# Four value units move from the value projection to the end of the head stage, and four groups of gates stand five units apart

## The chip, the cores and the metric

The kernel runs on one core of a Trainium2 chip. A core has TensorE (PE in the rows; its weight loads are PEld), VectorE (DVE), ScalarE (ACT), GpSimd (POOL) and SyncE (SP), each with its own instruction stream, which meet at semaphores, and 16 DMA engines. The metric is the device time of one execution in microseconds; lower is better.

## The reference, cut to what matters

Two transformer layers work on 16 sequences of 128 tokens with 512 features. In the first layer an mLSTM with 16 heads of 32 takes its queries from the normalised `x` and its keys and values from `ctx_2048`; its gates are products of the concatenated rows. A later attention takes keys and values from the same context:

```python
x = x + _L0_xattn_ref(_layernorm(x), ctx_2048, ctx_2048, Wi, bi, Wf, bf, ln_scale)   # mLSTM
    # ig = concat(q, k, v) @ Wi + bi ; fg = concat(q, k, v) @ Wf + bf
    # log_f_cum = cumsum(log_sigmoid(fg)) ; D = exp(... running maximum ...) ; h = (qk * D / norm) @ v
x = x + _L0_ffn_ref(_layernorm(x), ...)                                              # routed experts
x = x + _L1_xattn_ref(_layernorm(x), ctx_2048, ..., ki_w, vi_w, ...)                 # 16 heads of 128
    # k_img = rms_norm(ctx @ ki_w + ki_b) ; v_img = ctx @ vi_w + vi_b
x = x + _L1_ffn_ref(_layernorm(x), weight, bias)
```

The change touches where the values `ctx @ vi_w` of the second layer are multiplied, and the order in which the gates of the mLSTM are made.

## The kernel before, in words

The program is a chain of stages, each a block in which every engine has its own hand-ordered list; a block ends for all engines together. The first two stages are the ones that matter.

**values** (`values_and_gates`). The context is cut into four groups `g` of four sequences, the 2048 value columns into four quads `q`. A *value unit* is one sequence times one quad: four chunks of the 512 features, three matmuls each (lead by lead, lead by trail, trail by lead: a full-precision product out of two reduced halves), 12 matmuls of 128x512 into one of four banks. The list `FOURS` names the (quad, group) pairs done here: 13 of 16, so 52 units, `u` = 0 to 51. Two pairs are done much later (`DEFERRED`), and one, `TAIL` = quad 1 of group 3, at the end of the head stage. The loops of all engines run over `u`:

- PE makes the unit; in units 0 to 11 it also turns the context of the groups.
- ACT copies the product of even units (`keep_even`), DVE that of odd ones (`keep_odd`); PE takes a bank again four units later.
- SP loads the next quad's weights (`LOADS`, ten units before the quad opens); POOL writes their lead half (L370), DVE the trail half (`weight_trail`, `TRAILS`). A quad's first unit waits for all of it.
- The gates of group `g` begin at unit `GATES[g]` = 20, 26, 32, 38. With `at = u - GATES[g]`: PE turns chunk `at` of the normalised x (`turn_x`, L633) at 0 to 3, multiplies the context's part (`gates_ctx`, L644) at 0 and x's part of chunk `at - 1` (`gates_x`, L650 and L652) at 1 to 4. ACT makes two copies of each turned chunk (`xnT` at L439, `xl` at L442), DVE the trail half (`x_trail`, L501). At 5 ACT copies half of the gates' bank, DVE adds biases (`open_gates`, L508 and L509) and ACT takes abs, exp and ln; at 7 and 8 DVE scans (`decays`, `running`), which makes the running maximum that SP stores to memory (`running_max`, L333, at 9); at 11 PE turns two results (`natural`, L663).
- The x of a group is normalised by DVE three units before its gates (`normalise`, L493) into a buffer that all four groups share: it waits until PE has turned all four chunks of the group before.
- ACT's `xnT` also has one buffer: SP stores it (`xn_turned`, L326, at `GATES[g] + 4`), and the copy of the next group's first chunk waits until that store has landed. In SP's list the store stands behind the wait for the running maximum of the group before.

```python
for g in reversed(range(G)):                      # DVE, in each unit u
    at = u - GATES[g]
    if at == (-3 if g else -2): normalise(g)      # waits x_turned >= 4 * g
    if 0 <= at < C: x_trail(g * C + at)
```

**heads** (`heads_and_keys`). 64 steps of the mLSTM, and between them 64 *key units* of the second layer (12 matmuls each, L120 to L122 with `key_lead`). When the last scores are made, four key units are left (m = 12 to 15). Then PE makes three of `TAIL`'s four value units (`tail_unit`), whose weights were stored to memory in values and are loaded again, and then 16 column sums of the squared keys (L1361). ACT takes a square root of these sums (L1109) and behind it the root for the last rows' layer norm (L1111). Meanwhile DVE walks a long chain from the last head outputs to that layer norm. The next stage begins on PE with the fourth unit of `TAIL`.

Of the kernel before, what the change touches and what calls it, by code (L numbers as in the profile page):

```python
# [16 lines left out]
F32 = mybir.dt.float32  # L17
# [7 lines left out]
P = 128  # L25
B, S, D = 16, 128, 512
T = B * S
C = D // P
# [19 lines left out]
TAIL_BANKS = [0, 3, 1, 7]  # L48
TAIL_IN_HEADS = 3
LAST_LATE = []  # L50
LATE_BANKS = [2, 3, 0, 1]


# [20 lines left out]
class Phase:  # L74
# [26 lines left out]
    def sem(self, name):  # L101
        self.sems.append(self.nc.alloc_semaphore(name=f"{self.name}_{name}"))
        return self.sems[-1]
# [81 lines left out]
def values_and_gates(nc, K, M, A, E1, x_split, lead, trail, keep, a, v_dram, tail_dram, split_dram, xn_dram, ct_dram, g_dram):  # L185
    with Phase(nc, "values") as ph:
        sb, sem = ph.sb, ph.sem
        QUADS = H1 // 4
        FOURS = [(q, g) for q in range(QUADS) for g in range(G) if (q, g) not in DEFERRED + [TAIL] + LAST_LATE]
        OF = [(q, g * GB + b) for q, g in FOURS for b in range(GB)]  # L190
        UNITS = len(OF)
        OPENS = [OF.index((q, 0)) for q in range(QUADS)] + [UNITS]
# [43 lines left out]
        fmin_done, fabs_done, exp_done, sp_done = sem("fmin_done"), sem("fabs_done"), sem("exp_done"), sem("sp_done")  # L236
        m_done, em_done, nat_T, nat_done = sem("m_done"), sem("em_done"), sem("nat_T"), sem("nat_done")
        own_dve, own_pool = sem("own_dve"), sem("own_pool")
        tail_stored = sem("tail_stored")
        row_stats = RowStats(nc, K, ph)  # L240
        block = ph.block()
        ps = K.ps
# [5 lines left out]
        def _(sp):  # L248
# [37 lines left out]
            for u in range(UNITS):  # L286
# [17 lines left out]
                if u == OPENS[TAIL[0]] + 3:  # L304
                    sp.wait_ge(wt_done, (TAIL[0] + 1) * C)
                    for k, t in ((0, wl), (1, wt)):
                        sp.dma_start(tail_dram[k].rearrange("c p n -> p c n"), t[:, TAIL[0] % 2].bitcast(F32)
                                     ).then_inc(tail_stored, 16)
                if u in AHEAD_AT:
                    if u == AHEAD_AT[0]:  # L310
                        sp.wait_ge(x_product, (G - 1) * C + 1)
                        sp.wait_ge(split_stored, 2 * G * 16)
                        sp.wait_ge(product, OPENS[-2])
                        for pair in range(2):
                            A.load_raw(sp, pair)
                    for part in range(4):
                        A.load_split(sp, 0, 4 * AHEAD_AT.index(u) + part)
# [29 lines left out]
            store_four(len(FOURS) - 1)  # L347
            sp.wait_ge(stored[0], 16 * (len(FOURS) // 2))
            sp.wait_ge(tail_stored, 32)
            sp.wait_ge(split_stored, 2 * G * 16)  # L350
            sp.wait_ge(xT_stored, G * 16)
            sp.wait_ge(g_stored, G * 16)

        @block.gpsimd
        def _(pool):
            own = Own(pool, own_pool)
            nc.gpsimd.memset(w_gate[:], 0.0)
            nc.gpsimd.memset(bias[:], 0.0).then_inc(cleared, 1)
            nc.gpsimd.memset(keep[:], 1.0)
            own(nc.gpsimd.memset(pen[:], 0.0))  # L360
            nc.gpsimd.memset(keep[:, :, 0:1], 0.0)
            nc.gpsimd.memset(pen[:, :, 0:1], -FAR).then_inc(masks, 1)
            for q in range(1, QUADS):
                pool.wait_ge(raw_loaded, 16 * q)
                if q > 1:
                    pool.wait_ge(product, OPENS[q - 1])
                if q == TAIL[0] + 2:
                    pool.wait_ge(tail_stored, 32)
                for c in range(C):
                    nc.gpsimd.tensor_scalar(wl[:, q % 2, c, :], raw[:, c, :], 1.0, None, ALU.mult).then_inc(wl_done, 1)  # L370
            Phase.clear_over(nc)
# [10 lines left out]
        def _(act):  # L382
# [34 lines left out]
            for u in range(GB, UNITS):  # L417
# [9 lines left out]
                    nc.scalar.activation(w_x[:, :, 0, :], w_gate[:, 0], ACT.Copy).then_inc(wc_lead, 1)  # L427
                if u == NORMS + 1:
                    row_stats.root(act)
                for g in range(G):  # L430
                    at = u - GATES[g]
                    if 0 <= at < C:
                        s = g * C + at
# [150 lines left out]
        def _(pe):  # L584
# [90 lines left out]
            for u in range(GB, UNITS):  # L675
                if u + C < G * C:
                    turn(u + C)
                unit(u)
                for g in range(G):
                    at = u - GATES[g]  # L680
                    if 0 <= at < C:
                        turn_x(g, at)
                    if at == 0:
                        gates_ctx(g)
                    if 1 <= at <= C:
                        gates_x(g, at - 1)
                    if at == 11:
                        natural(g)


def tail_unit(nc, ps, split, tail_w, b):
    rows = slice(b * S, (b + 1) * S)
    for c in range(C):
        ins = three_passes(nc, ps[:, TAIL_BANKS[b], :], split[:, 1, 0, c, rows], split[:, 1, 1, c, rows], tail_w[:, 0, c],
                           tail_w[:, 1, c], c == 0, c == C - 1)
    return ins


def heads_and_keys(nc, K, M, A, E1, tail_dram, tail_w, tail_v, ctx_dram, ln_scale, xn_dram, ct_dram, g_dram, split_dram, b_dram, k_dram, rk):
# [28 lines left out]
    with Phase(nc, "heads") as ph:  # L728
# [36 lines left out]
        sums, rk_done = sem("sums"), sem("rk_done")  # L765
        csum_done, cmean_done, ht_done, quad_turned = sem("csum_done"), sem("cmean_done"), sem("ht_done"), sem("quad_turned")
        tail_loaded, tail_product, tail_kept = sem("tail_loaded"), sem("tail_product"), sem("tail_kept")
        held_act, held_pool, held_sp = sem("held_act"), sem("held_pool"), sem("held_sp")

        def after(g, n):  # L770
# [42 lines left out]
        def _(sp):  # L813
# [25 lines left out]
            def body(g, first, last=False):  # L839
                for n in range(PER):  # L840
# [26 lines left out]
                    if first and LAG <= n < LAG + 2 * C:  # L867
                        A.load_split(sp, 1, n - LAG)
                    if n == LAG and last:
                        sp.wait_ge(A.v_stored, 16 * ((H1 // 4 * G - len(DEFERRED)) // 2))  # L870
                        for w, at in zip(E1.weights, (0, C * F, 2 * C * F)):
                            rows = w.shape[0] // P
                            sp.dma_start(E1.raw[:, at:at + rows * w.shape[-1]].rearrange("p (c f) -> p c f", c=rows),
                                         w.rearrange("(c p) f -> p c f", p=P)).then_inc(E1.loaded, 16)
                        sp.dma_start(E1.wcol[:], E1.rms.rearrange("(c p) -> p c", p=P), allow_slow_non_contiguous=True
                                     ).then_inc(E1.small_loaded, 16)
                        sp.dma_start(E1.rw[:], E1.router.rearrange("(c p) e -> p c e", p=P)).then_inc(E1.small_loaded, 16)
                    keys_at(g, n, 1, next_raw, first)

            sp.wait_ge(qk, 4)  # L880
# [10 lines left out]
            sp.wait_ge(dec_done, UNITS)  # L891
            for k in range(2):
                sp.dma_start(tail_w[:, k].bitcast(F32), tail_dram[k].rearrange("c p n -> p c n")).then_inc(tail_loaded, 16)
            for k in range(2):
                sp.wait_ge(q_ring[k], 16 * (G * C // 2))
            for c in range(C):
# [106 lines left out]
        def _(act):  # L1003
# [74 lines left out]
            for g in range(1, G):  # L1078
                body(g, False)
            last = G - 1  # L1080
            for m in range(PER - LAG, PER + 1):
                if m < PER - LAG + 2:
                    weight_lead(last, m + 1)
                keep_key(last, m - 1)
                if m == PER - LAG:
                    row_sums(last)
                if m == PER - LAG + 1:
                    weight_lead(last, m + 2)
                    square(last, 0)
                    square(last, 1)  # L1090
                    act.wait_ge(early_agg, 1)
                    nc.scalar.activation(K.rstd[:, 0:EARLY], K.mv[:, 0:EARLY, 1], ACT.Sqrt, bias=K.eps5[:, 0:1]
                                         ).then_inc(early_root, 1)
                if m == PER - LAG + 3:
                    deviation(last)
                if m == PER:
                    act.wait_ge(early_ms, 1)
                    nc.scalar.activation(msq[:], msq[:], ACT.Sqrt, bias=K.eps6[:, 0:1]).then_inc(early_rms, 1)
# [191 lines left out]
        def _(pe):  # L1290
# [58 lines left out]
                body(g, False)  # L1349
            for m in range(PER - LAG, PER):  # L1350
                keys(G - 1, m)
            pe.wait_ge(tail_loaded, 32)
            pe.wait_ge(h_done, G * QUADS)
            tail_unit(nc, ps, split, tail_w, 0).then_inc(tail_product, 1)
            for b in range(1, TAIL_IN_HEADS):
                if TAIL_BANKS[b] in KEY_BANKS:
                    pe.wait_ge(ksq_done, UNITS)
                tail_unit(nc, ps, split, tail_w, b).then_inc(tail_product, 1)
# [197 lines left out]
def turned_and_shared(nc, K, R, E1, tail_w, tail_v, v_dram, lead, trail, normal, logits, rows_dram, gate_up_dram, rk, rk_dram):  # L1556
# [5 lines left out]
    with Phase(nc, "shared") as ph:  # L1562
# [165 lines left out]
        def _(act):  # L1728
# [4 lines left out]
            for u in range(G):  # L1733
# [5 lines left out]
                for f in range(FC):  # L1739
                    act.wait_ge(hid_done, 2 * u + f + 1)  # L1740
                    if u >= 2:
                        act.wait_ge(down, 4 * (u - 1))
                    nc.scalar.activation(hl[:, u % 2, f, :], hid[:, f, :], ACT.Copy).then_inc(hl_done, 1)

        @block.vector
# [1539 lines left out]
def two_layers(nc, a, out):  # L3285
# [12 lines left out]
    tail_dram = nc.dram_tensor("value_split", [2, C, P, N], F32).ap()  # L3298
    tail_w = nc.alloc_sbuf_tensor_at("tail_w", [P, 2, C, N], F32R, offset=TAIL_W)
    tail_v = nc.alloc_sbuf_tensor_at("tail_v", [P, 4, GB, DH1], F32, offset=TAIL_V)  # L3300
    x_split = (nc.alloc_sbuf_tensor_at("x_lead", [P, 2, N], F32R, offset=X_LEAD),
               nc.alloc_sbuf_tensor_at("x_trail", [P, N], F32R, offset=X_TRAIL))
    q_ahead = nc.alloc_sbuf_tensor_at("q_ahead", [P, 4, N], F32, offset=Q_AHEAD)
# [2 lines left out]
    with ExitStack() as stack:  # L3306
# [15 lines left out]
        with Phase(nc, "of_ffn") as outer:  # L3322
            with Phase(nc, "of_shared") as inner:
                E1 = first_ffn_operands(outer, inner, a)
                mlstm(nc, K, E1, x_split, a, tail_dram, tail_w, tail_v, v_dram, split_dram, ct_dram, k_dram, rk)
                with Phase(nc, "of_x1") as ph:
                    lead, trail = operands(ph)
# [40 lines left out]
```

## Time and profile before

| | us |
|---|---|
| median of 3 runs (lowest, highest) | 1348.18 (1343.0, 1348.6) |
| the profiled execution | 1345.04 |
| its span, first to last instruction | 1343.3 |
| PE busy | 1279.5 (95%) |
| DVE busy | 841.2 (63%) |
| ACT busy | 741.6 (55%) |

PE is the engine that has work nearly all the time, so a time is read from what PE does and waits for in each stage. A matmul of 128x512 is shown with a duration of 0.39 us, but they overlap; the distance from start to start counts. The values stage ends at 191.5 us, the head stage near 454.9 us. PEclk is the clock that TensorE was granted, as a share of 2.4 GHz; its lower level is one half.

### The profile page before, as it was taken

What the parts mean: (1) busy time and instruction counts of PE and PEld (TensorE: products, weight loads), DVE (VectorE), ACT (ScalarE), POOL (GpSimd) and SP (SyncE); (2) the same over time, 40 slices, a digit from 0 to 9 for tenths busy, and PEclk for the clock granted to TensorE, in tenths of its full rate; (3) what the DMA queues carried; (4) which work ended last, traced back from release to release, by engine and by line L of the source; (5) the groups of instructions that cost most, each with busy time, mean ns of one, the idle gap of its engine ahead of it and who ended that gap; (6) DMA issues with size and microseconds to landing.
All of it is one profiled execution on the core that took longest, in us unless ns stands there. A gap on an engine that the chain in (4) does not pass through costs nothing. (4 is left out here: it accounts for less than half of the span.)

```text
span 1343.3 us, 24403 instructions
## 1 busy us (share of the span) xinstructions
PE 1279.5 (95%) x7358; PEld 1059.4 (79%) x7359; DVE 841.2 (63%) x1613; ACT 741.6 (55%) x1831; POOL 379.5 (28%) x353
## 2 busy tenths in 40 slices
PE   7999997999999899899999989999989999999998
PEld 6787776777777778688877778878888888888986
DVE  3545546778779863644445477553577777777865
ACT  5225538787886431454455445445775655565561
POOL 0111014274737016399131342144010000000041
PEclk9999999999999899899999999999989999999999
DMA  7897399787864394666559776564475555555403
GB/s 255 290 365 255 139 317 322 268 265 253 280 223 166 88 345 174 223 180 208 148 170 314 255 261 189 158 210 172 143 213 166 160 157 167 159 162 157 120 28 126
DMA packets 166599, 277.06 MB, mean 206 GB/s; under 512 B 29744, under 2 KB 58160, under 8 KB 166256
## 3 DMA queue, kind: packets, MB, share of 16 engines
q1 hardware_dynamic: 140704, 220.50, 51.2%
q0 software_dynamic: 8672, 29.37, 6.7%
q10 hardware_dynamic: 17136, 26.09, 5.3%
q8 instruction: 47, 0.77, 0.2%
q14 instruction: 40, 0.33, 0.1%
HBM read 167.11 MB, written 108.80 MB: 205 GB/s over the span
## 5 line engine op out<-in xcount | busy, mean ns | idle before, releaser
L120 PE MATMUL banks<-of_shared_split,key_lead 128*128 128x512 f32 x256 | 104.7, 409 | 11.5 <-DVE key_trail L1403 10.1
L2984 ACT ACTIVATE prob<-banks,attend_row,rq 128x128 f32<-128x128 f32 x248 | 110.5, 470 | 0.0
L2997 ACT ACTIVATE attend_ol<-banks,of_attend_vbias 128x512 fp32r<-128x512 f32 x64 | 44.2, 691 | 117.0 <-PE banks L3196 117.0
L120 PE MATMUL banks<-wo,attend_ol 128*128 (+1 forms) x256 | 106.2, 415 | 0.0
L120 PE MATMUL banks<-queries_rows_split,queries_wl 128*128 128x512 f32 x256 | 100.8, 394 | 0.0
L122 PE MATMUL banks<-wo,attend_ot 128*128 (+1 forms) x256 | 100.7, 393 | 0.0
L122 PE MATMUL banks<-of_shared_split,key_trail 128*128 128x512 f32 x256 | 100.6, 393 | 0.0
L121 PE MATMUL banks<-of_shared_split,key_lead 128*128 128x512 f32 x256 | 100.1, 391 | 0.0
L121 PE MATMUL banks<-wo,attend_ol 128*128 (+1 forms) x256 | 99.9, 390 | 0.0
L122 PE MATMUL banks<-queries_rows_split,queries_wt 128*128 128x512 f32 x256 | 99.8, 390 | 0.0
L121 PE MATMUL banks<-queries_rows_split,queries_wl 128*128 128x512 f32 x256 | 99.7, 390 | 0.0
L2966 POOL TENSOR_TENSOR x_kept<-x_kept,attend_tern_bias 128x512 f32<-128x512 f32 x12 | 15.5, 1294 | 282.6 <-ACT of_attend_raw L3023 281.0
L2634 DVE TENSOR_TENSOR queries_total<-queries_total,queries_sq 128x512 f32<-128x512 f32 x60 | 45.0, 751 | 75.2 <-ACT queries_sq L2547 75.2
L2543 ACT ACTIVATE queries_head<-banks,queries_bias 128x512 f32<-128x512 f32 x64 | 44.1, 689 | 81.7 <-PE banks L122 76.1
L1013 ACT ACTIVATE heads_dec<-mlstm_gmax,mlstm_nat 128x128 f32<-128x128 f32 x256 | 81.3, 389 | 10.0 <-POOL mlstm_gmax L921 4.8
L120 PE MATMUL banks<-of_shared_split,of_ctx_lead 128*128 128x512 f32 x208 | 84.0, 404 | 2.0 <-DVE of_ctx_trail L480 1.8
L1198 DVE TENSOR_TENSOR heads_total<-heads_total,heads_ksq 128x512 f32<-128x512 f32 x60 | 56.6, 943 | 42.1 <-ACT heads_ksq L1055 41.8
L122 PE MATMUL banks<-of_shared_split,of_ctx_trail 128*128 128x512 f32 x208 | 82.3, 396 | 0.0
L3085 DVE TENSOR_TENSOR x_kept<-x_kept,banks 128x512 f32 (+1 forms) x64 | 44.0, 688 | 60.8 <-PE banks L122 60.2
L121 PE MATMUL banks<-of_shared_split,of_ctx_lead 128*128 128x512 f32 x208 | 81.7, 393 | 0.0
L3177 PEld LDWEIGHTS banks<-attend_kn,q_ahead 128*128 128x128 f32 x496 | 66.0, 195 | 6.2 <-issue 1.9
L120 PEld LDWEIGHTS banks<-of_shared_split,key_lead 128*128 128x128 f32 x256 | 48.1, 188 | 28.5 <-DVE key_trail L1403 14.9
(399 smaller groups left out, 3535.0 us busy)
## 6 DMA issues: line engine op xcount, KB each, us to landing
mlstm_gmax<-running_max SPq DMA_DIRECT2D x32, 512.0 KB, 6.2
k_heads<-heads_key ACTq DMA_DIRECT2D x64, 256.0 KB, 4.4
q_heads<-queries_head SPq DMA_DIRECT2D x64, 256.0 KB, 2.6
q_ahead<-q_heads SPq DMA_DIRECT2D x64, 256.0 KB, 4.2
of_attend_k<-k_heads SPq DMA_DIRECT2D x60, 256.0 KB, 4.1
of_attend_v<-v_heads SPq DMA_DIRECT2D x60, 256.0 KB, 3.2
key_raw<-in_L_xattn_ki_w SPq DMA_DIRECT2D x20, 512.0 KB, 5.5
sorted_rows<-of_shared_split SPq DMA_DIRECT2D x2, 5120.0 KB, 27.6
```

What stands on the lines that cost most here:

```text
L120: nc.tensor.matmul(out, lead_l, lead_r, start=first, stop=False)
L121: nc.tensor.matmul(out, lead_l, trail_r, start=False, stop=False)
L122: return nc.tensor.matmul(out, trail_l, lead_r, start=False, stop=last)
L1013: ins = nc.scalar.activation(dec[:, n % 2, b], gmax[:, h // 2 % 4, h % 2 * N + b * S:h % 2 * N + (b + 1) * S], ACT.Exp, scale=-1.0, bias=M ...
L1198: nc.vector.tensor_tensor(t, t, ksq[:, m % 2, :], ALU.add).then_inc(total_done, 1)
L2543: nc.scalar.activation(head[:, u % HEADS_RING, :], ps[:, u % 4, :], ACT.Identity, bias=bias[:, h:h + 1]).then_inc(head_done, 1)
L2634: nc.vector.tensor_tensor(t, t, sq[:, u % 2, :], ALU.add).then_inc(total_done, 1)
L2966: nc.gpsimd.tensor_tensor(K.x[:, b, :], K.x[:, b, :], tern_bias[:], ALU.add).then_inc(tern_bias_done, 1)
L2984: ins = nc.scalar.activation(prob[:, j % 2, b, :], ps[:, j % 2, b * S:(b + 1) * S], ACT.Exp, bias=row[:, j % 2, 1, b:b + 1], scale=rq[:, b ...
L2997: nc.scalar.activation(ol[:, par, j, :], ps[:, 4 + j % 2, :], ACT.Identity, bias=vbias[:, bass.ds(quad_of(it) * 4 + j, 1)]).then_inc(ol_do ...
L3085: nc.vector.tensor_tensor(xb, xb, ps[:, 6 + b % 2, :], ALU.add).then_inc(acc_done, 1)
L3177: ins = nc.tensor.matmul(ps[:, j % 2, s], q[:, j, s], kn[:, j % 2, s], start=True, stop=True)
```

## The change

The pair `SECOND` = quad 0 of group 3 leaves `FOURS`: 48 units are left in values, quads open at 0, 12, 24 and 36, and `GATES`, which is worked out from the number of units, becomes 20, 25, 30, 35. The split weights of quad 0 are stored to memory at unit 12, loaded again in the last group of heads, and PE makes the four units one behind each of the last four key units. `gates_ctx` moves from `at == 0` to `at == 1`; ACT walks the groups downwards, so the copies of the next group's first chunk come ahead of the step `at == 5` of the group before. The lines of DVE are the same.

```diff
+SECOND = (0, G - 1)
+SECOND_W, SECOND_V = 98848, 203296
+SECOND_BANKS = [2, 3, 4, 5]
@@ values @@
-        FOURS = [(q, g) for q in range(QUADS) for g in range(G) if (q, g) not in DEFERRED + [TAIL] + LAST_LATE]
+        FOURS = [(q, g) for q in range(QUADS) for g in range(G) if (q, g) not in DEFERRED + [TAIL, SECOND] + LAST_LATE]
@@ values, SP @@
+                if u == OPENS[SECOND[0] + 1]:
+                    sp.wait_ge(wt_done, (SECOND[0] + 1) * C)
+                    for k, t in ((0, wl), (1, wt)):
+                        sp.dma_start(E1.second_dram[k].rearrange("c p n -> p c n"), t[:, SECOND[0] % 2].bitcast(F32)
+                                     ).then_inc(second_parked, 16)
@@ values, POOL @@
+                if q == SECOND[0] + 2:
+                    pool.wait_ge(second_parked, 32)
@@ values, ACT @@
-                for g in range(G):
+                for g in reversed(range(G)):
@@ values, PE @@
-                    if at == 0:
+                    if at == 1:
                         gates_ctx(g)
@@ heads, SP @@
+                    if last and n == PER - 4:
+                        sp.wait_ge(qk, UNITS)
+                        sp.wait_ge(ctx1_done, G)
+                        for k in range(2):
+                            sp.dma_start(E1.second_w[:, k].bitcast(F32), E1.second_dram[k].rearrange("c p n -> p c n")
+                                         ).then_inc(second_loaded, 16)
...
+            sp.wait_ge(second_kept, GB)
+            qs, gs = SECOND
+            sp.dma_start(E1.v_dram[qs * 4:qs * 4 + 4, :, gs * GB:(gs + 1) * GB, :].rearrange("h l b e -> l h (b e)"),
+                         E1.second_v[:].rearrange("p h b e -> p h (b e)")).then_inc(E1.second_stored, 16)
@@ heads, ACT @@
+            def keep_second(b):
+                act.wait_ge(second_product, b + 1)
+                if b == 0:
+                    act.wait_ge(pv, G * QUADS)
+                nc.scalar.activation(E1.second_v[:, :, b, :], ps[:, SECOND_BANKS[b], :].rearrange("p (h e) -> p h e", h=4),
+                                     ACT.Copy).then_inc(second_kept, 1)
+
             for m in range(PER - LAG, PER + 1):
                 if m < PER - LAG + 2:
                     weight_lead(last, m + 1)
                 keep_key(last, m - 1)
+                if m > PER - LAG:
+                    keep_second(m - 1 - PER + LAG)
@@ heads, PE @@
             for m in range(PER - LAG, PER):
                 keys(G - 1, m)
+                if m == PER - LAG:
+                    pe.wait_ge(second_loaded, 32)
+                    pe.wait_ge(c_done, UNITS)
+                tail_unit(nc, ps, split, E1.second_w, m - PER + LAG, SECOND_BANKS).then_inc(second_product, 1)
             pe.wait_ge(tail_loaded, 32)
             pe.wait_ge(h_done, G * QUADS)
             tail_unit(nc, ps, split, tail_w, 0).then_inc(tail_product, 1)
+            pe.wait_ge(second_kept, 2)
```

The shared feed-forward stage behind waits once for `second_stored`.

## Rows read from the trace of the kernel before

**Rows 1.** Waits of PE from 0 to 225 us: total, times, longest us

```profile
PE banks L120 <- DVE of_ctx_trail L480: 1.8, 1, 1.8
...
PE banks L650 <- ACT x_lead L442: 0.8, 1, 0.8
PE banks L652 <- DVE x_trail L501: 0.6, 2, 0.4
```

**Rows 2.** Timeline of PE, first matmuls of units 13 and 14: start, duration us

```profile
56.49 0.39 PE L120 MATMUL banks<-of_shared_split,of_ctx_lead 128*128 128x512 f32 x1
...
59.23 0.39 PE L120 MATMUL banks<-of_shared_split,of_ctx_lead 128*128 128x512 f32 x1
```

**Rows 3.** Three stretches: length, busy us (x instructions), granted clock, DMA share, GB/s

```profile
core 0: us, PE busy (x) PEld busy (x) DVE busy (x) ACT busy (x) POOL busy (x), PEclk, DMA share, GB/s
50.22:55.60 5.38, 3.56 (x9) 2.79 (x10) 5.38 (x10) 0.60 (x1) 3.22 (x3) 0.70 1.04 393
200.74:207.00 6.26, 3.02 (x16) 2.25 (x16) 3.05 (x5) 5.80 (x16) 4.85 (x8) 1.00 0.95 294
446.40:451.71 5.31, 5.31 (x32) 5.22 (x32) 5.24 (x4) 0.18 (x1) 0.00 (x0) 0.68 0.00 0
```

**Rows 4.** Timelines of SP and POOL: the weights of quad 1

```profile
33.92 1.05 SPq L290 DMA_DIRECT2D mlstm_gmax<-in_L_xattn_vi_w  x1
...
47.57 5.87 POOL L370 TENSOR_SCALAR of_shared_split<-mlstm_gmax 128x512 fp32r<-128x512 f32 x4 [43.48 <-DMA mlstm_gmax<-in_L_xattn_vi_w]
```

**Rows 5.** Timelines of PE, ACT and DVE: last chunk of the first gates

```profile
90.79 0.60 PE L633 MATMUL banks<-ident,mlstm_kT 128*128 128x128 f32 x4
...
91.46 0.39 PE L652 MATMUL banks<-x_trail,values_w_x 128*128 128x512 f32 x1
...
94.76 0.50 PE L652 MATMUL banks<-x_trail,values_w_x 128*128 128x512 f32 x1
...
91.49 0.60 ACT L439 ACTIVATE mlstm_gmax<-banks 128x512 f32<-128x512 f32 x1 [2.56 <-PE banks L633]
...
92.20 1.91 DVE L493 TENSOR_SCALAR mlstm_kT<-x_kept,mv,rstd 128x512 f32<-128x512 f32 x4
94.02 0.68 DVE L501 TENSOR_TENSOR x_trail<-banks,x_lead 128x512 fp32r<-128x512 f32 x1
```

**Rows 6.** Timelines of DVE, ACT and SP: the steps of later gates

```profile
122.27 0.73 DVE L508 SCALAR_TENSOR_TENSOR values_irow<-banks,values_bias,values_w_gate 32x512 f32<-32x512 f32 x1
...
123.79 0.63 ACT L454 ACTIVATE values_f_abs<-values_w_gate 32x512 f32<-32x512 f32 x1 [4.26 <-DVE values_w_gate L509]
...
127.75 0.62 ACT L439 ACTIVATE mlstm_gmax<-banks 128x512 f32<-128x512 f32 x1
...
128.89 0.69 DVE L501 TENSOR_TENSOR x_trail<-banks,x_lead 128x512 fp32r<-128x512 f32 x1 [3.94 <-ACT x_lead L442]
...
175.19 0.67 DVE L518 TENSOR_TENSOR values_f_min<-values_f_min,values_f_abs 32x512 f32<-32x512 f32 x1
...
179.81 0.32 SPq L333 DMA_DIRECT2D running_max<-values_grow  x1
```

**Rows 7.** Issue to landing, 1024 KB each: the xn_turned stores (L326), then the value stores (L283)

```profile
DMA to landing us min/median/max: 6.4/7.6/9.9
...
DMA to landing us min/median/max: 4.2/5.7/13.1
```

**Rows 8.** Timelines of PE and ACT at the end of heads

```profile
424.48 0.48 PE L120 MATMUL banks<-of_shared_split,key_lead 128*128 128x512 f32 x1
...
437.38 0.39 PE L120 MATMUL banks<-tail_w,of_shared_split 128*128 128x512 f32 x1
...
446.40 5.31 PE L1361 MATMUL banks<-ones,heads_total 128*128 128x1 f32 x32 [0.45 <-DVE heads_total L1198]
454.93 0.76 PE L120 MATMUL banks<-tail_w,of_shared_split 128*128 128x512 f32 x1 [3.22 <-PEq L86]
...
451.75 0.27 ACT L1109 ACTIVATE rk<-banks,eps 128x16 f32<-128x16 f32 x1 [5.17 <-PE banks L1361]
454.16 0.30 ACT L1111 ACTIVATE rstd<-mv,eps 128x4 f32<-128x4 f32 x1 [2.14 <-DVE mv L1284]
```

More of the change, by code:

```diff
@@ L238, in values_and_gates @@
         own_dve, own_pool = sem("own_dve"), sem("own_pool")
-        tail_stored = sem("tail_stored")
+        tail_stored, second_parked = sem("tail_stored"), sem("second_parked")
         row_stats = RowStats(nc, K, ph)
@@ L349, in _ @@
             sp.wait_ge(tail_stored, 32)
+            sp.wait_ge(second_parked, 32)
             sp.wait_ge(split_stored, 2 * G * 16)
@@ L688, in _, with tail_unit @@
                         natural(g)
-def tail_unit(nc, ps, split, tail_w, b):
+def tail_unit(nc, ps, split, tail_w, b, banks=TAIL_BANKS):
     rows = slice(b * S, (b + 1) * S)
     for c in range(C):
-        ins = three_passes(nc, ps[:, TAIL_BANKS[b], :], split[:, 1, 0, c, rows], split[:, 1, 1, c, rows], tail_w[:, 0, c],
+        ins = three_passes(nc, ps[:, banks[b], :], split[:, 1, 0, c, rows], split[:, 1, 1, c, rows], tail_w[:, 0, c],
                            tail_w[:, 1, c], c == 0, c == C - 1)
@@ L767, in heads_and_keys @@
         tail_loaded, tail_product, tail_kept = sem("tail_loaded"), sem("tail_product"), sem("tail_kept")
+        second_loaded, second_product, second_kept = sem("second_loaded"), sem("second_product"), sem("second_kept")
         held_act, held_pool, held_sp = sem("held_act"), sem("held_pool"), sem("held_sp")
@@ L869, in body @@
                     if n == LAG and last:
-                        sp.wait_ge(A.v_stored, 16 * ((H1 // 4 * G - len(DEFERRED)) // 2))
+                        sp.wait_ge(A.v_stored, 16 * ((H1 // 4 * G - len(DEFERRED) - 1) // 2))
                         for w, at in zip(E1.weights, (0, C * F, 2 * C * F)):
@@ L1742, in _ @@
                         act.wait_ge(down, 4 * (u - 1))
+                    elif u == 0 and f == 0:
+                        act.wait_ge(E1.second_stored, 16)
                     nc.scalar.activation(hl[:, u % 2, f, :], hid[:, f, :], ACT.Copy).then_inc(hl_done, 1)
@@ L3300, in two_layers @@
     tail_v = nc.alloc_sbuf_tensor_at("tail_v", [P, 4, GB, DH1], F32, offset=TAIL_V)
+    second_dram = nc.dram_tensor("second_split", [2, C, P, N], F32).ap()
+    second_w = nc.alloc_sbuf_tensor_at("second_w", [P, 2, C, N], F32R, offset=SECOND_W)
+    second_v = nc.alloc_sbuf_tensor_at("second_v", [P, 4, GB, DH1], F32, offset=SECOND_V)
     x_split = (nc.alloc_sbuf_tensor_at("x_lead", [P, 2, N], F32R, offset=X_LEAD),
@@ L3324, in two_layers @@
                 E1 = first_ffn_operands(outer, inner, a)
+                E1.second_dram, E1.second_w, E1.second_v, E1.v_dram = second_dram, second_w, second_v, v_dram
+                E1.second_stored = inner.sem("second_stored")
                 mlstm(nc, K, E1, x_split, a, tail_dram, tail_w, tail_v, v_dram, split_dram, ct_dram, k_dram, rk)
```

## The prediction

> **What bounds the kernel now.** I read the page first: PE has work nearly all the time, so where PE already runs without gaps, work taken out comes back in full, and where it idles, work put in is free. Then PE's waits in the values stage. They are few: 1.8 us ahead of unit 12, and 0.8 and 0.6 us in the gates [rows 1]; the rest is dense, and a unit costs 59.23 - 56.49 = 2.74 us [rows 2]. (The 0.39 us of a matmul overlap; twelve of them in 2.74 us are the full clock.) So the four units are worth 4 x 2.74 = 11.0 us where they are now. Next the end of heads. PE makes keys and tail units up to 446 us, the column sums until 451.7, and idles until the next stage at 454.93 [rows 8]. There ACT's root for the layer norm at 454.16 waited for DVE, not for the sums, whose own root was free at 451.75: the idle room in front of the stage's end is some 3 us, not 11. Last, the gates in the timelines, since their distance shrinks.
>
> **The change, part by part.**
>
> *Units out of values*: -11.0 us, as above.
>
> *The wait ahead of unit 12.* Unit 12 waits for the last trail half of the context. DVE was late with it because the weights of quad 1, issued at 33.92, landed only at 47.57, behind three other transfers of 1 MB, and DVE's lists go on in order [rows 4]. In the 5.38 us from 50.22 PE worked 3.56 at a mean clock of 0.70: 1.82 us idle at full clock, the rest at 0.54, which loses 3.56 x 0.46 = 1.6 [rows 3]. After the change unit 12 belongs to quad 1 and needs its weights; they are issued at u = 2 instead of 6, ahead of those three transfers, some 3.6 us earlier. At a quarter of the 13.65 us that the four together took, they land near 34 to 37, POOL's 5.87 us end by 43, and DVE, whose list has to wait for the first x in between, ends near 47, 3 us before unit 12. So I take the whole wait away: -3.5. If DVE is later, it stays: 0.
>
> *Parking the weights* adds two 1 MB stores, two 1 MB loads and moves one value store. The stores go out at unit 12 and PE waits for none of them; POOL does, before quad 2, whose weights are behind them anyway. The loads are issued once the scores end, near 406 us, and are needed at 427. Nothing: 0, up to 2 if quad 2's weights hold DVE's `normalise(0)`, which is next in its list.
>
> *Five units between gates.* This is the part that I think costs most. `normalise(g+1)` stays three units before its gates, which is now `at` = 2 of group g, while the turn that it waits for is at 3. DVE stands in front of `x_trail(g, 2)` until PE has turned chunk 3, and PE's next pair of matmuls behind this turn is the one that needs `x_trail(g, 2)`. In the rows the turn starts at 90.79 and its reader ACT at 91.49 (0.70); `normalise` to `x_trail` is 94.02 - 92.20 = 1.82; `x_trail` to its matmul 94.76 - 94.02 = 0.74. So the matmul comes 3.26 us after the turn; before it came 91.46 - 90.79 = 0.67 after [rows 5]. 2.6 us of idle PE, three times: +7.8. Nothing stands between the two PE instructions that could cover it.
>
> *What is late next.* `decays` and `running` of group g-1 are behind it on DVE, and the store of `xn_turned` of group g is behind their result on SP; ACT's first copy for group g+1 waits for that store, formerly with a unit more to spare. Counted from the turn of chunk 3 of group 1: `x_trail` at 0.70 + 1.82 = 2.52; `decays` 0.60 later; from `decays` to SP's store of the maximum 179.81 - 175.19 = 4.62, and another `x_trail` of 0.60 between: 8.3; the next issue 0.4 behind it, 8.7. Landing: stores of this kind took 6.4 to 9.9 us, but with others ahead; the value stores of the same size go down to 4.2 [rows 7], and little is under way here, so I take 4.2: 12.9. From ACT's copy to `x_trail` is 128.89 - 127.75 = 1.14, `x_trail` itself 0.6, the two bias steps up to ACT's abs 123.79 - 122.27 = 1.52 [rows 6]: the gates' bank is free at 16.2. PE comes to `gates_ctx(2)` after 3.5 (the late matmul and its 0.23), three units (8.2), a turn and a gate pair (0.67 + 0.23 = 0.9 by [rows 5]), another turn (0.36) and `natural`, eight small turns that I take as two of those (0.7): 13.7. Wait 2.5. For group 3 the same sum with `keep_odd` and `weight_trail` (0.6 each) also on DVE gives 17.4 against 14.8: 2.6. For group 1 no maximum is ahead of the store, but 2 to 4 MB of context halves are: about 1.0. Together +6.1. It would be 0.5 if the copies were never held, and +12 at landings of 7.6.
>
> *Waits that stay.* The 1.4 us of [rows 1] in the gates come again as some 2.2: ACT's exp and ln in front of a copy (1.0), and `x_trail(2, 3)` behind six DVE steps (1.2). +0.8. Values in all: -11.0 - 3.5 + 7.8 + 6.1 + 0.8 = +0.2: the stage ends where it did.
>
> *Units into heads.* Key unit 12 starts at 424.48 as before. Then four key units (2.74) and seven value units ((446.40 - 437.38 - 0.45) / 3 = 2.8 at most) [rows 8] put the sums at 424.48 + 11.0 + 19.6 = 455.1. Key and value units in turn close the small waits for key weights that were there. DVE's chain hardly moves: it waits for squares of keys that come up to 8 us later, but ACT, not PE, set most of those; by the list ACT's `keep_second(2)` holds `deviation` 0.9 us, of which DVE feels 0.3. So the sums, 2 us ahead of DVE's chain before, are now 6 us behind it, and the root for the layer norm is queued behind theirs on ACT: 455.1 + 5.35 + 0.25 = 460.7, and the next stage 0.77 later (as 454.16 to 454.93) at 461.5. +6.5.
>
> *Clock.* The gap of 1.82 us was followed by half clock, the gap of 3.24 us at 200.74 was not: the window of 6.26 us has 1.00 [rows 3]. Five new gaps of 2.5 us, half of them followed by 1.6 us of loss, would be +4; part falls into the next wait, which PE's own speed doesn't set. +2, bounds 0 and +8. The Trainium skill (TensorE: Matmul & The Clock Gate, on HAM oscillation) has idle gaps lower the clock only from a length that all these gaps stay under, so by that rule the term is 0 and the sum 2 us less; the short gap in rows 3 speaks against the rule. In the sums the clock fell to a mean of 0.68 [rows 3]; at full clock they take 5.31 x 0.68 = 3.6, so -1.7 is possible, and as much again in the slow unit behind. I take 0, since the sums look the same.
>
> **Sum**: +0.2 + 6.5 + 2 = +8.7 on the profiled execution's 1345.0: 1353.7. The median of the runs is 3.1 above that execution, so 1357 for a median.
>
> **Rivals.**
> - *Five apart costs no more than six* (the other side): the gates' waits stay at 1.4. Then -11.0 - 3.5 + 6.5 = -8, 1340. It decides at new gate waits of 1.3 us in all. For it: the waits were small so far. Against it: the order of DVE's list, which the change leaves.
> - *Only `normalise` binds*: the stores land in time and the clock holds. -11.0 - 3.5 + 7.8 + 0.5 + 0.8 + 6.5 = +1, 1349. For it: a lone transfer may land earlier than any in rows 7.
> - *Everything collides*: the wait ahead of unit 12 stays (+3.5), stores land at 7.6 (+6), half clock after each gap (+4 more): +22; with half of it +15, 1363. For it: DMA share 1.04 in that window [rows 3].
> - *The change doesn't move the bound*: the units go, but DVE or DMA set the pace of values, and nothing is gained there; for this nothing speaks but the wait of [rows 1]. +7 to +10, within my range.
>
> **How the numbers follow.** My forecast 0.55, only `normalise` 0.18, everything collides 0.17, no cost of five 0.10. 0.5% is 6.7 us, about what a measurement of this kernel can tell from no change. Of the forecast (+4 to +13) I put 0.39 above 6.7 us; with the collision that is 0.56 slower. Same: 0.16 of the forecast and 0.18 of the second rival, less a little, 0.34. Faster 0.10. The range leaves out the rival on the other side and the worst collision: 1346 to 1367; the forecast's own is 1352 to 1361.
>
> **What would show it.** Right: PE's waits between 75 and 180 us list `x_trail` three times at 2.6 us and DVE's bias step or ACT some 2.5 us ahead of `gates_ctx`; no wait ahead of unit 12; values end at 190 to 193 us; the sums start near 455, and ACT's L1111 waits for PE's sums, not for DVE. Wrong: the values stage ends before 185 us, or the next stage starts less than 4 us later relative to the values' end, or a new wait for weights stands at units 12 or 24.

## The result, and the profile after

The changed kernel takes 1360.98 us (median of 4 runs, 1358.21 to 1363.51), the kernel before in the same runs 1348.39 (1343.0 to 1351.64): a ratio of 1.0107, 95% interval 1.0082 to 1.0132. The forecast was 1357, range 1346 to 1367, with slower as the likeliest. The profiled execution of the changed kernel took 1359.66 us against 1345.04, a span longer by 14.7 us.

Where the 14.7 us lie is read from two marks on PE. The first score matmul of the heads starts at 193.84 us before and at 201.77 after; I call this the end of the values. The first matmul of the stage behind the heads starts at 454.93 [rows 8] and at 468.17. So the values take 7.9 us more, the stretch behind them 266.40 in place of 261.09, 5.3 more, and the rest 1.5. The two first score matmuls, before and after:

```profile
193.84 1.17 PE L1300 MATMUL banks<-mlstm_q,mlstm_kT 32*128 32x128 f32 x32 [2.40 <-PEq L86]
...
201.77 1.32 PE L1332 MATMUL banks<-mlstm_q,mlstm_kT 32*128 32x128 f32 x32 [2.40 <-PEq L89]
```

PE's waits from 0 to 225 us in the changed kernel (engine, tile and line, what it waited for: us in total, times, longest):

```profile
PE banks L663 <- DVE x_trail L512: 7.6, 4, 2.7
...
PE banks L655 <- DVE values_w_gate L520: 4.1, 3, 2.1
PE banks L123 <- DVE of_ctx_trail L491: 3.1, 1, 3.1
...
PE banks L661 <- ACT x_lead L453: 0.3, 1, 0.3
```

These four lines sum to 15.1 us, where the three of [rows 1] have 3.2: 11.9 us more. The stretches right behind the six larger gaps (length, busy us and number of instructions of PE, PEld, DVE, ACT and POOL, granted clock, DMA share, GB/s):

```profile
41.05:45.35 4.30, 4.30 (x12) 3.25 (x13) 2.80 (x5) 1.20 (x2) 2.58 (x2) 0.64 1.05 391
95.36:99.83 4.47, 4.47 (x14) 3.54 (x15) 1.23 (x2) 0.00 (x0) 0.00 (x0) 0.67 0.67 242
120.70:125.38 4.68, 4.68 (x13) 3.74 (x14) 4.54 (x6) 0.00 (x0) 0.00 (x0) 0.64 0.01 4
148.24:152.83 4.59, 4.59 (x13) 3.65 (x14) 4.49 (x7) 0.00 (x0) 0.00 (x0) 0.65 0.01 4
162.69:167.50 4.81, 4.81 (x21) 3.98 (x22) 0.48 (x2) 4.64 (x7) 0.00 (x0) 1.00 0.21 64
...
134.89:139.50 4.61, 4.61 (x14) 3.75 (x15) 2.15 (x4) 4.14 (x6) 0.00 (x0) 0.68 0.40 153
```

Each begins where a gap ended. In five of the six PE is busy all the time and yet slow, since most of its matmuls run at half clock; length times (1 - clock) is 1.55 + 1.48 + 1.68 + 1.61 + 1.48 = 7.8 us. Before, this loss was 1.6 us, at unit 12 [rows 3]. The values then close as units -11.0, waits +11.9, clock +6.2: +7.1 of the 7.9 measured.

The gap ahead of x's trail half, in the timelines of PE and DVE (start, duration, engine, line, and in brackets the idle time before and its releaser):

```profile
92.15 0.60 PE L644 MATMUL banks<-ident,mlstm_kT 128*128 128x128 f32 x4
92.50 0.48 PE L661 MATMUL banks<-x_lead,values_w_x 128*128 128x512 f32 x1
95.36 0.50 PE L663 MATMUL banks<-x_trail,values_w_x 128*128 128x512 f32 x1 [2.37 <-DVE x_trail L512]
...
92.79 1.92 DVE L504 TENSOR_SCALAR mlstm_kT<-x_kept,mv,rstd 128x512 f32<-128x512 f32 x4 [6.09 <-PE banks L644]
94.62 0.68 DVE L512 TENSOR_TENSOR x_trail<-banks,x_lead 128x512 fp32r<-128x512 f32 x1
```

DVE stood idle for 6.09 us in front of `normalise` (L504) until PE turned the last chunk at 92.15; `x_trail` came behind it, and PE had nothing else to do. In [rows 5] the same turn is followed by the gate matmul after 0.67 us, here after 3.21.

Unit 8, in the timelines of POOL, DVE and PE:

```profile
37.77 5.86 POOL L381 TENSOR_SCALAR of_shared_split<-mlstm_gmax 128x512 fp32r<-128x512 f32 x4 [33.67 <-DMA mlstm_gmax<-in_L_xattn_vi_w]
...
39.30 1.09 DVE L496 TENSOR_TENSOR of_shared_split<-mlstm_gmax,of_shared_split 128x512 fp32r<-128x512 f32 x1 [5.58 <-POOL of_shared_split L381]
40.31 0.68 DVE L491 TENSOR_TENSOR of_ctx_trail<-banks,of_ctx_lead 128x512 fp32r<-128x512 f32 x1
...
41.05 0.50 PE L123 MATMUL banks<-of_shared_split,of_ctx_lead 128*128 128x512 f32 x1 [3.15 <-DVE of_ctx_trail L491]
```

The weights of quad 1 land near 37.7, some 10 us earlier than in [rows 4]. But DVE's list now meets their first trail half (L496) at unit 6, and the trail half of the context (L491) that unit 8 needs stands behind it. The wait of unit 12 was not removed; it went to unit 8 and grew from 1.8 to 3.15 us.

The store, in the timelines of SP, ACT and PE:

```profile
125.90 0.32 SPq L341 DMA_DIRECT2D running_max<-values_grow  x1
126.27 0.42 SPq L334 DMA_DIRECT2D xn_turned<-mlstm_gmax  x1
...
131.51 0.60 ACT L450 ACTIVATE mlstm_gmax<-banks 128x512 f32<-128x512 f32 x1 [2.12 <-DMA xn_turned<-mlstm_gmax]
...
117.20 0.60 PE L644 MATMUL banks<-ident,mlstm_kT 128*128 128x128 f32 x4
...
134.89 0.77 PE L655 MATMUL banks<-of_ctx_lead,values_w_ctx 128*128 128x512 f32 x1 [1.75 <-DVE values_w_gate L520]
```

It is issued 0.37 us behind the maximum of the group before and lands 5.2 us later; ACT waits for that, DVE's bias step (L520) comes behind ACT, and PE gets the gates' bank only behind that step. The turn at 117.20 is that of chunk 3 of group 1, from which the prediction counted.

The end of the heads, on PE and ACT:

```profile
462.73 4.30 PE L1398 MATMUL banks<-ones,heads_total 128*128 128x1 f32 x32
468.17 0.76 PE L123 MATMUL banks<-tail_w,of_shared_split 128*128 128x512 f32 x1 [1.15 <-PEq L89]
...
467.06 0.27 ACT L1141 ACTIVATE rk<-banks,eps 128x16 f32<-128x16 f32 x1 [3.54 <-PE banks L1398]
467.23 0.29 ACT L1143 ACTIVATE rstd<-mv,eps 128x4 f32<-128x4 f32 x1
```

ACT's root of the sums waits for PE, as it did before. But the layer norm's root, which before waited 2.14 us more for DVE [rows 8], now has nothing left to wait for and follows right behind it: PE's sums, not DVE's chain, set the end.

### The profile page after: what moved, and what is told of

Same layout as the page of the kernel before. It is cut to its first block and busy times, and to the rows that moved or that the text cites. A ratio compares the mean times of both kernels' runs of the same rounds, so it can differ in the third digit from the quotient of the medians.

```text
span 1358.0 us, 24409 instructions
## 1 busy us (share of the span) xinstructions
PE 1286.1 (95%) x7358; PEld 1065.6 (78%) x7359; DVE 844.0 (62%) x1611; ACT 743.1 (55%) x1833; POOL 377.9 (28%) x353
## 5 line engine op out<-in xcount | busy, mean ns | idle before, releaser
L123 PE MATMUL banks<-of_shared_split,of_ctx_lead 128*128 128x512 f32 x192 | 79.5, 414 | 3.4 <-DVE of_ctx_trail L491 3.1
L125 PE MATMUL banks<-of_shared_split,of_ctx_trail 128*128 128x512 f32 x192 | 77.7, 405 | 0.0
L124 PE MATMUL banks<-of_shared_split,of_ctx_lead 128*128 128x512 f32 x192 | 76.9, 400 | 0.0
L123 PE MATMUL banks<-routed_w,routed_lead 128*128 x156 | 65.1, 417 | 4.8 <-DVE routed_trail L2222 4.5
```

The source lines that it names most:

```text
L123: nc.tensor.matmul(out, lead_l, lead_r, start=first, stop=False)
L124: nc.tensor.matmul(out, lead_l, trail_r, start=False, stop=False)
L125: return nc.tensor.matmul(out, trail_l, lead_r, start=False, stop=last)
```

## The experiments

All ratios are to the kernel before, in the same runs; each label's columns are read from its own profile. One caution: the fifth kernel leaves the values as the changed kernel has them, and yet its profile ends them at 205.45 and not 201.77. Ends of values from single profiles can differ by some 4 us, so each is read with its gaps and its ratio. The columns `x_trail` and `gates_ctx` are PE's waits, in total, ahead of the products with x's trail half and ahead of the gates' bank (for DVE's bias step); all times are in us.

| kernel | wait, unit 8 or 12 | `x_trail` | `gates_ctx` | values end | stretch behind | ratio, 95% |
|---|---|---|---|---|---|---|
| before | 1.8 | 0.6 | - | 193.84 | 261.09 | 1 |
| changed | 3.1 | 7.6 | 4.1 | 201.77 | 266.40 | 1.0107 (1.0082, 1.0132) |
| 1 normalise later | 3.6 | 2.3 | 6.1 | 197.80 | 267.46 | 1.0043 (1.0013, 1.0073) |
| 2 trails later | - | 8.2 | 6.2 | 198.89 | 265.51 | 1.0081 (1.0051, 1.0112) |
| 3 store ahead | 3.5 | 8.7 | 2.1 | 200.48 | 267.24 | 1.0049 (1.0023, 1.0075) |
| 4 before, five apart | 1.9 | 7.3 | 5.0 | 211.51 | 260.28 | 1.0156 (1.0115, 1.0196) |
| 5 short units | 4.2 | 7.6 | 5.4 | 205.45 | 262.96 | 1.0064 (1.0039, 1.0090) |
| 6 three together | - | 2.0 | 3.7 | 187.07 | 269.33 | 1.0002 (0.9983, 1.0020) |
| 7 before, trails later | - | 0.6 | - | 190.69 | 263.04 | 0.9976 (0.9956, 0.9997) |
| 8 six apart, from 17 | 9.1 | 0.8 | - | 190.82 | 267.43 | 1.0013 (0.9995, 1.0032) |
| 9 gates 18, 24, 30, 35 | 2.9 | 3.8 | 0.3 | 189.75 | 269.08 | 1.0004 (0.9984, 1.0024) |
| 10 six apart, later | 3.7 | 0.8 | - | 189.16 | 268.64 | 1.0026 (1.0005, 1.0046) |
| 11 all mended | 0.7 | 0.6 | 0.3 | 179.86 | 265.06 | 0.9915 (0.9887, 0.9942) |

**1.** `normalise` of groups 1 to 3 one unit later.

```diff
-                    if at == (-3 if g else -2):
+                    if at == -2:
```

> The changed kernel, with DVE's normalise of the next group one unit later (two units ahead of its gates), so that it stands behind x_trail of chunk 2 again. Theory (the order of DVE's list makes the gaps): PE's three gaps of 2.4, 2.7 and 2.4 us ahead of gates_x go, and with them the half clock of about 1.5 us behind each; the running maximum comes some 3 us earlier against PE's 2.5, so the two gaps ahead of gates_ctx stay near 2 us. About -12 us against the changed kernel: 1349, values end near 187 instead of 199. Rival (the gaps only move to gates_x of chunk 3): within 3 us of 1361. Rival (the units in heads cost it all): 1361, gaps or not.

The `x_trail` gaps fall from 7.6 to 2.3 us, so they came from that order. Only a part of the expected 12 us arrives, some 8.6 by the ratios and 4.0 by the ends of the values in single profiles: the waits in front of `gates_ctx` grow to 6.1, since ACT still waits for the store.

```profile
121.03 0.42 SPq L334 DMA_DIRECT2D xn_turned<-mlstm_gmax  x1
...
126.28 0.60 ACT L450 ACTIVATE mlstm_gmax<-banks 128x512 f32<-128x512 f32 x1 [3.53 <-DMA xn_turned<-mlstm_gmax]
```

**2.** The trail halves of quad 1's weights one unit later in DVE's list (offset 5 in place of 6 for `q == 0` in `TRAILS`).

> The changed kernel, with DVE's four trail halves of quad 1 in units 7 to 10 instead of 6 to 9, so that the first stands behind the last context half that unit 8 needs. Theory (a wait in DVE's list): PE's gap of 3.15 us ahead of unit 8 goes, and the slow stretch of some 1.5 us behind it: -4.6, 1356.4. Rival (DVE is late as a whole, the gap moves on to unit 12, as it moved from 12 to 8): within 1 us of 1361, with a gap of 2 to 3 us at unit 12.

The wait of unit 8 goes and none comes at unit 12; the first gap in the gates ends at 90.95 in place of 95.36, 4.4 us earlier as expected. Behind it the gates' waits take part of it back (14.4 us for 11.7), and the ratio's interval overlaps with that of the changed kernel: the cause is shown, the gain alone is not.

**3.** SP issues the store of the tokens ahead of the maximum of the group before.

```diff
-                for g in range(G):
+                for g in reversed(range(G)):
```

> The changed kernel, with SP's store of the turned x of a group ahead of, not behind, its wait for the running maximum of the group before. Theory (ACT's copy is held by that store): ACT no longer waits for the landing, the gaps of 1.75 and 2.07 us ahead of gates_ctx shrink to 0.3, the first of them loses its half clock as well: -4 to -5, 1356.5. The three gaps ahead of gates_x stay at 2.4 to 2.7. Rival (ACT or DVE hold the gates' bank by their own work): within 1 us of 1361.

The `gates_ctx` waits halve, 4.1 to 2.1, and ACT's copy is no longer held by the store. What is left are the bias steps on DVE, which there wait 1.3 us for PE's own small turns (`natural`). The `x_trail` gaps stay, as they should (8.7 for 7.6).

**4.** The kernel before with all 52 units, and only the gates 5 apart, with `gates_ctx` one unit later and ACT's groups in reverse, as the change has them.

> The kernel before, with its 52 units in values and nothing moved to heads, and only the gates five units apart, gates_ctx at the second unit and ACT's downward order. Theory (the spacing itself costs): three gaps of 2.4 to 2.7 us with half clock behind, two of about 2 us ahead of gates_ctx, less the 1.4 us of waits there now: +12 to +16 against the kernel before, 1362. Rival (spacing is free, the units in heads cost): within 2 us of 1348.

```profile
PE banks L652 <- DVE x_trail L501: 7.3, 4, 2.4
PE banks L644 <- DVE values_w_gate L509: 5.0, 3, 3.3
...
PE banks L120 <- DVE of_ctx_trail L480: 1.9, 1, 1.9
```

The same two groups of gaps stand there, with no unit moved; unit 12's wait is the one of before. The spacing, with the two changes of order that go with it, costs 17.7 us of the values in this profile, and 1.56% or 21 us of the whole, above the 12 to 16 expected. The two changes of order were not run alone; with 6 units between the gates (8 and 11) they open no gap.

**5.** The four moved units with 3 of their 12 matmuls each.

```diff
-    for c in range(C):
+    chunks = range(C) if banks is TAIL_BANKS else range(C - 1, C)
+    for c in chunks:
...
```

> The changed kernel, but each of the four moved units in the heads does 3 of its 12 matmuls (three of the four feature chunks of those units' values are left out); copies, loads and stores stay. In the changed kernel the stretch from the end of the values (201.77) to the first matmul of the next stage (468.17) takes 266.4 us, before 261.1 (193.84 to 454.93). Theory: behind the key units the way to the end is shared by TensorE and VectorE, so taking 36 matmuls (36 x 0.23 = 8.4 us) away brings back only about 5.6 us, and the stretch takes 260 to 262. Rival 1: TensorE alone sets it, the stretch takes 258. Rival 2: the loads and the store of the moved units set it, and it stays at 266. Against the kernel before the whole is then about +7 us (ratio 1.005) by the theory, +4 by rival 1, +13 by rival 2.

The stretch is 262.96, 3.4 us less for 8.4 us of PE's work. That is nearest to the theory (the rivals are off by 5 and 3), but two kernels without the moved units differ among themselves by 2.8, so the size of the two shares is only roughly known. Which engine ends the stage is plain from the profile:

```profile
468.41 0.77 PE L123 MATMUL banks<-tail_w,of_shared_split 128*128 128x512 f32 x1 [4.79 <-PEq L89]
```

With the short units PE idles 4.79 us ahead of the next stage, and ACT's root for the layer norm waits 3.71 us for DVE again: what PE gives back beyond that point, DVE's chain keeps.

**6.** The edits of 1, 2 and 3 together.

> The changed kernel with the three edits that were run alone, together: the normalising of groups 1 to 3 one unit later, the low parts of the second quad's weights one unit later, and the store of a group's normalised tokens issued ahead of the earlier group's running maxima. Alone they moved the end of the values from 201.77 to 197.80, 198.89 and 200.48. Theory 1: the waits stand in one chain, and each edit alone left the next wait to take up most of it, so together they bring more than the sum: the values end at or before 188, and the time is within 0.5% of the kernel before or better (1338 to 1349). Theory 2: the three are independent, the values end at 201.77 - 4.0 - 2.9 - 1.3 = 193.6, and with the 5.8 us of the heads the kernel is 5 to 6 us slower than before (ratio 1.004). Rival: the spacing of 5 units itself holds the work between groups, and the values do not end before 197.

Values end at 187.07 and the ratio is 1.0002, within theory 1. The profiles gain 14.7 us where the three alone gained 8.1. By the ratios, though, the three alone sum to 0.0064 + 0.0026 + 0.0058 = 0.0148 and bring 0.0105 together. So the waits do not simply add, but whether they stand in one chain is not settled.

**7.** The kernel before with the edit of 2 alone.

> The kernel before, and only the low parts of the second quad's weights one unit later in VectorE's order. Theory: the wait ahead of unit 12 before (3.5 us) has the same cause as the wait ahead of unit 8 after (3.15 us): in VectorE's order the first low part of the weights, which waits for POOL and so for the load, stands ahead of the low part of the tokens that the next unit needs. Then the wait ahead of unit 12 falls below 1 us, the values end 3 to 4 us earlier (190 to 191) and the ratio is 0.997. Rival: the load itself is late and the wait only moves by a unit: values end within 1 us of 193.84, ratio 1.000.

No wait of `of_ctx_trail` is left, values end 3.15 us earlier, and the ratio is 0.9976: the wait of unit 12 before and of unit 8 after have one cause.

**8.** The changed kernel with `GATES` at 17, 23, 29, 35 and the statistics (`STATS`, `NORMS`) two units earlier.

> The changed kernel with its four units in the heads, but the gates of two groups stay 6 units apart: they begin at unit 17 in place of 20, and the token statistics at 6 in place of 8. Theory: the waits around the gates (7.6 us in front of the x parts, 4.1 us in front of the context parts, about 4 us of half clock behind them) come from the spacing, so with 6 units they shrink to the kernel before's 0.6 us and little else: the values end at 188 to 191 and the whole is within 0.5% of the kernel before (ratio 0.997 to 1.002). Rival 1: it is the units gone, less work on TensorE against the same chain of transfers, that opens the waits, whatever the spacing: the values end at 197 or later. Rival 2: three units earlier the gates meet the stores of the turned context and wait for them: the first group's wait is over 4 us, the later ones are gone.

```profile
PE banks L123 <- DVE of_ctx_trail L491: 9.1, 1, 9.1
...
PE banks L663 <- DVE x_trail L512: 0.8, 3, 0.4
...
PE banks L661 <- ACT x_lead L453: 0.3, 1, 0.3
```

With 6 units the gates' waits are gone (1.1 us in all), though four units are missing: rival 1 falls. The time in the forecast band is an accident, because the earlier statistics opened a new wait. DVE's list meets them at unit 6 and stands until the tokens have landed at 45.01, with the context's trail half behind them:

```profile
38.84 1.09 DVE L496 TENSOR_TENSOR of_shared_split<-mlstm_gmax,of_shared_split 128x512 fp32r<-128x512 f32 x1 [5.15 <-POOL of_shared_split L381]
45.01 1.29 DVE L140 BATCH_NORM_STATS2 stats<-x_kept 128x6 f32<-128x512 f32 x2 [5.08 <-DMA x_kept<-in_x]
46.21 0.67 DVE L491 TENSOR_TENSOR of_ctx_trail<-banks,of_ctx_lead 128x512 fp32r<-128x512 f32 x1
```

**9 and 10.** The statistics one unit early, the edit of 2, and `GATES` at 18, 24, 30, 35 (9) or 17, 23, 29, 35 (10).

> The changed kernel with gates at units 18, 24, 30 and 35, the token statistics from unit 7, and the low parts of the second quad's weights one unit later. Theory: both causes are then gone but for one group at 5 units: no wait over 1 us ahead of unit 8, a gap of some 2 us ahead of the x parts and of the context parts of the last group only, and the values end at 182 to 185 (from 190.82 with the wait of 9.08 us and its half clock that six units apart showed). With 6 to 8 us more in the heads the ratio to the kernel before is 0.995 to 0.999. Rival 1: the loads of the tokens and of the weights land late whatever the order, and a wait of over 4 us stands somewhere before unit 12: values end at 188 or later, ratio 1.000 or more. Rival 2: the spare time only moves into the heads (end of values 183, but the stretch behind it 272 or more in place of 266): ratio 1.000.

> As the kernel with 18, 24, 30 and 35, but gates at 17, 23, 29 and 35, all 6 apart, with one unit less between the statistics and the first group. Theory: no gap at 6 units, but the first group's normalising now waits for the statistics' root: one wait of up to 4 us ahead of the first turn of x and no other over 1 us, so the values end at 182 to 186. Rival: the first group's late start is handed on and gaps of over 2 us stand at each group: values end at 192 or later, ratio 1.002 or more.

Both theories fell. Unit 12 waits 2.9 and 3.7 us for the weights, whose trail halves now stand behind the statistics and so behind the tokens. By its end and its ratio kernel 9 lies in rival 1, but not by its cause: the wait is below 4 us and comes of the order, since it is 0.7 us in 11 with the statistics one unit later. The 2.37 us gap at the one spacing of 5 in kernel 9 is as expected. In kernel 10 the first turn of x waits 2.85 us, as expected, but the values end 3 us later than thought.

**11.** The edits of 6, with gates at 18, 24, 30, 35 and the statistics where they were.

> The changed kernel with the three edits together (normalising later, low parts of the weights later, store of the tokens first) and gates at units 18, 24, 30 and 35, the statistics where they were. The three edits alone ended the values at 187.07 with 6.1 us of waits around the gates. Theory: 6 units apart take most of these away, the first group waits for its normalising (up to 3 us, as with gates from 17), and the values end at 182 to 184; the heads then take the 267 to 269 us that the kernels with the moved units showed, against 261 to 263 without, and the ratio to the kernel before is 0.995 to 0.999. Rival: the stretch behind the values takes up what the values save (272 or more), and the ratio stays at 1.000.

```profile
PE banks L123 <- DVE of_shared_split L496: 0.7, 1, 0.7
PE banks L663 <- DVE x_trail L512: 0.6, 2, 0.4
PE banks L644 <- DVE mlstm_kT L504: 0.3, 1, 0.3
PE banks L655 <- DVE values_w_gate L520: 0.3, 1, 0.3
```

The values end at 179.86, 13.98 us before those of the kernel before, and the mean clock from 95 us on is 1.00. The ratio is 0.9915: faster than both kernels, clear of the noise. It is more than expected, since the values end 2 us before the band and the stretch behind is 265.06, 2 us below the band; why the stretch is short here was not looked into. Not all of it is due to the move: the edit of 2 alone gives the kernel before 0.9976 (7), so the move with the other edits is worth some 0.6%.

## Why the prediction was right or wrong

- *Units out, -11.0*: right. Kernel 11 has no gap above 0.7 us and no slow stretch: the units' -11.0, waits 1.9 for 3.2 and no clock loss for 1.6 make -13.9, measured -13.98.
- *The wait ahead of unit 12: "So I take the whole wait away: -3.5."* This step failed. I followed the weights to unit 12 and found DVE done in time there, but did not ask which earlier unit stands behind the moved `weight_trail` in DVE's list. It is unit 8: 3.15 us and a slow stretch, measured in the changed kernel and removed by 2.
- *Five apart, `normalise`, +7.8*: 2.37 + 2.66 + 2.37 = 7.4. Shown by 1, 4 and 8.
- *Store and `gates_ctx`, +6.1*: 0.29 + 1.75 + 2.07 = 4.1, with the mechanism as told (3). The store ahead of group 1 landed in time. For group 2 the way to the bank was longer than summed: the store landed in 5.2 us and not 4.2, and the bank was free 17.7 us after the turn (117.20 to 134.89) and not 16.2. But PE itself came 15.9 us after it and not 13.7, for 1.68 us of half clock lay on its way, so the wait was 1.75 and not 2.5. This loss fell into the wait.
- *Waits that stay, +0.8*: of the 1.4 us of before 0.5 are left (0.2 of `x_trail`, 0.3 of `x_lead`), so -0.9.
- *Clock, "+2, bounds 0 and +8"*: the mis-sized term. With the 1.6 us counted off at unit 12, my net was +0.4; it is +6.2. I let half of the gaps be followed by a slow stretch and part of that vanish; five of six were, and what vanished shows as the shorter waits at the store. The Trainium skill (TensorE: Matmul & The Clock Gate, on HAM oscillation) has idle gaps lower the clock only from a length that all six gaps here stayed under. By that rule this term is 0, and the trace does not agree: five of the six, of 1.75 to 3.15 us, were followed by a mean clock of 0.64 to 0.68.
- *Units into heads, +6.5*: +5.3 here. Over all runs, the nine kernels with whole moved units have a mean of 267.35 and the three without them 261.47: +5.9. Single profiles of the nine lie between 265.06 and 269.33, and why is open. The new order on ACT is as forecast.
- *Parking, 0*: right as far as seen; PE waits for no weights at the later quads nor for the moved units' weights.

The forecast of the values was +2.2 with the clock, measured +7.9: 5.7 of the 6.0 us by which the profiled execution missed 1353.7. The sum of idle waits, 12.8 forecast (7.8 + 6.1 + 0.8 - 1.9) against 11.9, was close by luck: unit 8 made up for the shorter waits at the store and for the small ones that went. Of the rivals, "everything collides" came nearest, by its half: a wait of that kind stayed, at unit 8, and half clock followed nearly every gap, but the stores did not land at 7.6. Of the signs, the gaps ahead of `x_trail` and `gates_ctx` and the root behind PE's sums came; the values' end did not (190 to 193 by the stage's last matmuls, measured 201.77 - 2.40 = 199.4), nor did sums near 455 (462.73).

## What to carry to other kernels

When work leaves a pipelined stage, every step placed by unit number moves against the steps that are placed by data: go through each in-order list and ask what now stands in front of what. The move itself was worth the time, but only once three orders and the spacing were mended; with PE free of gaps and at full clock all of it gave 0.85%. Price a new gap on TensorE as its idle time plus a stretch of half clock behind it: in the changed kernel 1.5 to 1.7 us, behind five gaps of six, and nothing where that stretch falls into a wait that PE does not set.

## What the runs showed of the hardware

In the values stages of the changed kernel and of experiments 1 to 6 and 8 to 10, PE has 36 gaps of 1.43 us or more between 30 us and its last value matmul. Read over the 4.6 us behind each, the granted mean was 0.50 to 0.69 after 29, that is largely at 1.2 GHz, and 1.00 (2.4 GHz) after 7. Of nine gaps of 0.91 to 1.35 us none was. The length doesn't decide alone: of twelve gaps of 2.37 us, nine were followed by half clock. Two of them stand in one execution, that of experiment 2, behind 90.95 and 143.79 us:

```profile
90.95:95.55 4.60, 4.59 (x20) 3.79 (x21) 1.24 (x2) 0.60 (x1) 0.00 (x0) 1.00 0.68 248
143.79:148.39 4.60, 4.60 (x14) 3.62 (x15) 4.50 (x7) 0.00 (x0) 0.00 (x0) 0.64 0.02 4
```

In the first, 20 matmuls are made in the time of 14. What makes the difference stays open. Nor does each slow stretch cost time. The gap of 2.40 us ahead of the first score matmul stands in all 13 kernels, and the 4.6 us behind it have a mean of 0.50 to 0.68 in nine of them (0.63 in the changed kernel) and of 1.00 in four (the kernel before among them). Yet PE's next wait, for the keys' trail half, ends 10.13 us behind that matmul in the changed kernel and 10.14 in the kernel before; it is 1.69 us long in the one and 3.25 in the other, so the loss fell into a wait that PE does not set.
